# The norm ahead of an FFN in two halves, the output projection in an order that suits it, and the next chunk's gate and up products ahead of the LoRA products

## The reference

```python
x = x + attention(layernorm(x), ctx)          # 16 heads of 32, causal; "x1" below
h = layernorm(x)
logits = h @ W_router                         # 8 experts, top 2 -> weights w (rows x 8)
gate = h @ W_gate + lora(h, sA_gate, sB_gate) + expert_lora(h, A_gate, B_gate, w)
up   = h @ W_up   + lora(h, sA_up, sB_up)     + expert_lora(h, A_up, B_up, w)
hidden = silu(gate) * up                      # 1376 columns, padded to 11 chunks of 128
x = x + hidden @ W_down + lora(...) + expert_lora(...)   # "x2"
x = x + softmax(layernorm(similarity(layernorm(x), ctx)))  # "x3"
x = x + sparse_ffn(layernorm(x))              # 64 experts, top 8
```

## Time and profile before

| | us |
|---|---|
| median of 3 runs | 1436.13 (1434.3 to 1439.93) |
| the profiled execution's own time | 1430.09 |
| its span in the profile | 1428.3 |
| PE busy | 1220.8 |
| DVE busy | 742.1 |
| ACT busy | 504.6 |
| POOL busy | 503.5 |

### The profile page before, as it was taken

The page is one execution under the profiler, slowest core; times in us unless marked ns, Lnnn a source line. Parts: engine busy times, 40 slices in busy tenths (PEclk is TensorE's granted clock), DMA queues, the critical chain, the costliest instruction groups (busy, mean ns, idle before and its releaser), DMA issues. The chain is left out here.

```text
span 1428.3 us, 19290 instructions
## 1 busy us (share of the span) xinstructions
PE 1220.8 (85%) x6510; PEld 891.9 (62%) x6510; DVE 742.1 (52%) x1427; ACT 504.6 (35%) x1145; POOL 503.5 (35%) x533
## 2 busy tenths in 40 slices
PE   0788999887999987799998779999349999999990
PEld 0567777655777765577776557777145666666660
DVE  6674645576576658568666847443641222222220
ACT  1681322565322167422216643121222233323320
POOL 2520333633033373303346330221005455555541
PEclk9999999998999999899999999999658999999995
DMA  7002221000242100033200002641417999999957
GB/s 263 1 1 91 81 108 54 0 1 31 91 141 81 54 1 1 31 115 116 107 28 1 1 31 114 233 153 42 199 68 247 338 338 353 355 348 359 276 85 132
DMA packets 45600, 181.07 MB, mean 127 GB/s; under 512 B 6412, under 2 KB 9484, under 8 KB 36692
## 3 DMA queue, kind: packets, MB, share of 16 engines
q1 hardware_dynamic: 30660, 140.23, 26.2%
q0 software_dynamic: 14864, 39.85, 12.2%
HBM read 149.36 MB, written 34.90 MB: 129 GB/s over the span
## 5 line engine op out<-in xcount | busy, mean ns | idle before, releaser
L2001 PE MATMUL PS<-WE,XGT 128*128 128x384 f32 x512 | 195.2, 505 | 1.5 <-DVE HM L1577 0.8
L656 POOL CAST HH<-HID 128x512 fp32r<-128x512 f32 x44 | 34.0, 773 | 343.2 <-DVE HID L1483 343.2
L786 ACT ACTIVATE P<-PS,NM 128x512 f32<-128x512 f32 (+3 forms) x256 | 132.0, 534 | 50.4 <-DVE NM L1194 49.2
L1600 PE MATMUL PS<-XTH,WHI 128*128 128x512 f32 x352 | 142.9, 406 | 1.0 <-ACT SIL L929 1.0
L1436 DVE TENSOR_TENSOR WLO<-WRAW,WHI 128x584 fp32r<-128x584 f32 (+1 forms) x88 | 109.7, 1247 | 62.8 <-ACT WHI L915 57.0
L1601 PE MATMUL PS<-XTL,WHI 128*128 128x512 f32 x352 | 140.3, 399 | 0.0
L1602 PE MATMUL PS<-XTH,WLO 128*128 128x512 f32 x352 | 140.3, 399 | 0.0
L915 ACT ACTIVATE WHI<-WRAW 128x1280 fp32r<-128x1280 f32 x44 | 56.2, 1277 | 207.0 <-DMA WRAW<-in_ffn 204.1
L2001 PEld LDWEIGHTS PS<-WE,XGT 128*128 128x128 f32 x512 | 88.2, 192 | 57.8 <-issue 23.5
L1194 DVE TENSOR_REDUCE NM<-PS 128x2 f32<-128x1024 f32 (+2 forms) x96 | 98.6, 1041 | 44.8 <-PE PS L1609 44.3
L1660 PE MATMUL PS<-ident,P 128*128 128x128 f32 x640 | 97.5, 289 | 22.8 <-ACT P L786 12.8
(11 more groups left out here) (269 smaller groups left out, 2748.0 us busy)
## 6 DMA issues: line engine op xcount, KB each, us to landing
WE<-in_we SPq DMA_DIRECT2D x64, 1152.0 KB
WRAW<-in_ffn SPq DMA_DIRECT2D x44, 932.0 KB, 4.6
acc<-HN SPq DMA_DIRECT2D x17, 256.0 KB, 4.6
XIN<-in_x SPq DMA_DIRECT2D x4, 1024.0 KB, 9.2
out<-X SPq DMA_DIRECT2D x4, 1024.0 KB, 4.2
out<-acc POOLq DMA_DIRECT2D x1, 4096.0 KB, 23.3
hx<-HN SPq DMA_DIRECT2D x3, 1152.0 KB, 8.7
CTX<-in_ctx SPq DMA_DIRECT2D x4, 256.0 KB, 6.7
```

Source lines behind the costliest of these rows:

```text
L786: act.activation(prob(t, n), PS[:, c0:c0 + (t + 1) * P], ACT.Exp, bias=NM[:, c:c + 1], accum_out=SSUM[:, c:c + 1]).then_inc(S["p_ready"], 1)
L1600: pe.matmul(dst, a[0], b_[0], start=first, stop=False, **kw)
L2001: mm = pe.matmul(bank(2 + s % 2, 0, 2 * F1), XGT[s % 2][:, k, :], WE[s][:, k * 2 * F1:(k + 1) * 2 * F1], start=(k == 0), stop=(k == KC - 1))
```

## The change

1. *Output projection.* PE makes pieces 0 to 2 of tiles 0, 1, 2, the context product, piece 3 of these three, the keys' transposition, and then tile 3 whole.
2. *Norm in two halves.* DVE sums and takes statistics for tiles 0 and 1 and posts their variances, then for tiles 2 and 3. POOL raises each half to -1/2 and normalises its two tiles itself (`first_norm`). The norms of a batch count 5 instead of 4.
3. *Head of the FFN.* The transposed tiles go to banks 6, 7, 4, 5. PE interleaves transposes and projections. DVE subtracts chunk 0's weights between tiles 1 and 2.
4. *Chunk 1.* Its gate and up products go to banks 4 and 5 and stand ahead of the LoRA products of chunk 0; both chunks' LoRA products follow. Its weights are split before. Banks 6, 7, 2 are zeroed behind them, banks 4 and 5 within `down(0)`, which takes tiles 2, 3, 0, 1 and waits for chunk 1's HID in between.
5. *Loads and side work.* SP loads chunks 0 and 1 as soon as attention's last product is made. The next batch's front work goes to chunks 2, 3 and 4, 5, 6, 8; `gates_rest` goes behind chunk 1.

```diff
+NORMS = 5
+TURNED_BANK = (6, 7, 4, 5)
+GATE_BANK, UP_BANK = {1: 4}, {1: 5}
+    FRONT_Q = (4, 5, 6, 8)
...
                 sp.wait_ge(S["pv_ps"], 1 + G * (b + 1))
                 alone(sp, "sp")
-                sp.wait_ge(S["x1_ready"], 1 + NT * (b + 1))
-                alone(sp, "sp")
                 sp.dma_start(WRAW[0][:, :], w["ffn"][0:P, :]).then_inc(w_loaded[0], 16)
                 sp.dma_start(WRAW[1][:, :], w["ffn"][P:2 * P, :]).then_inc(w_loaded[1], 16)
                 if not last:
+                    sp.wait_ge(S["x1_ready"], 1 + NT * (b + 1))
                     sp.wait_ge(S["ctxT_ps"], 1 + b + 1)
...
+            def power(b, n, t0=0, t1=NT):
+
+                pool.wait_ge(S["norm_in"], 1 + NORMS * b + n)
+                pool.tensor_tensor(sm[1][:, t0:t1], sm[0][:, t0:t1], mhalf[:, t0:t1], ALU.pow).then_inc(S["norm_out"], 1)
...
+            def first_norm(a):
+
+                for n, (t0, t1) in ((1, (0, 2)), (2, (2, 4))):
+                    power(a, n, t0, t1)
+                    normed(a, n, XN, "xn_ready", t0, t1)
...
-                        if i == 0 and not last:
-                            front_power(b + 1, d)
-                    if not last:
-                        front_q(b + 1, i)
+                        f = 2 * i + d
+                        if f in (2, 3) and not last:
+                            front_power(b + 1, f - 1)
+                        if f in FRONT_Q and not last:
+                            front_q(b + 1, FRONT_Q.index(f))
...
+                act.wait_ge(S["op_ps"], 1 + NT * b + 1)
+                wg_hi(0, 0, b * N0 + 1)
                 act.wait_ge(S["op_ps"], 1 + NT * (b + 1))
...
-                wg_hi(0, 0, b * N0 + 1)
...
                 def chunk(f, slot, next_loads):
 
-                    if next_loads is not None:
+                    if next_loads is not None and f > 1:
                         act.wait_ge(S["up_ps"], 1 + b * NF + f)
                         wg_hi(f + 1, 1 - slot, next_loads)
...
                     silu(f)
+                    if f == 1:
+                        act.wait_ge(S["up_ps"], 1 + b * NF + 1)
+                        wg_hi(2, 0, next_loads)
+                wg_hi(1, 1, b * N1 + 1)
...
                 dve.wait_ge(S["out_stored"], 16 * (a + 1))
-                stats(row_x, x1, "x1_ready", NT * a)
-                variances(a, 1, EPS_LN)
-                normed(a, 1, XN, "xn_ready")
-                dve.wait_ge(S["xn_ready"], 1 + NT * (a + 1))
+                for t0, n in ((0, 1), (2, 2)):
+                    x1(t0)
+                    x1(t0 + 1)
+                    stats_x1(t0)
+                    step.need(stats_x1(t0 + 1))
+                    aggregate(t0, t0 + 2)
+                    variances(a, n, EPS_LN, t0, t0 + 2)
...
+                turned_rest(0)
+                turned_rest(1)
                 w_rest(0, 0, 0, WD, "wg_hi", "wg_lo")
+                turned_rest(2)
+                turned_rest(3)
...
+                w_rest(1, 1, 0, WD, "wg_hi", "wg_lo")
                 for h in range(2):
                     dve.wait_ge(S["lx_hi"], 1 + 2 * b + h + 1)
...
                 chunk(0, 0)
+                chunk(1, 1)
                 if b > 0:
                     gates_rest(b - 1)
...
+                pe.wait_ge(S["oT_lo"], 1 + (G - 1) * (a + 1))
+                for t in range(NT - 1):
+                    if t == 1:
+                        inverse(G - 1)
+                    projected_out(t, 0, KC - 1)
+                pe.wait_ge(S["ctxT_sb"], 1 + a + 1)
+                pe.matmul(bank(0), wk[:, :], UN[:, :], start=True, stop=True).then_inc(S["kvT_ps"], 1)
+                pe.wait_ge(S["oT_last_lo"], 1 + a + 1)
+                for t in range(NT - 1):
+                    projected_out(t, KC - 1, KC).then_inc(S["op_ps"], 1)
                 pe.wait_ge(S["kv_act"], 1 + a + 1)
                 for t in range(NT):
                     mm = pe.transpose(bank(0, t * P, (t + 1) * P), KVT[:, t * P:(t + 1) * P], ident[:, :])
                 mm.then_inc(S["kv_ps"], 1)
+                projected_out(NT - 1, 0, KC).then_inc(S["op_ps"], 1)
...
+                turned(0)
+                turned(1)
+                projection(0)
+                turned(2)
+                projection(1)
+                turned(3)
+                projection(2)
+                projection(3)
...
-                    for t in range(NT):
+                    for t in (2, 3, 0, 1):
+                        if f == 0 and t == 0:
+                            pe.wait_ge(S["hid_ready"], 1 + b * NF + 2)
+                            clear(4, 5)
...
+                gate_up(1, 1, "weights")
                 pe.wait_ge(S["lx_lo"], 1 + 2 * (b + 1))
                 gate_up(0, 0, "lora")
-
-                for bk in (4, 5, 6, 7, 2):
-                    pe.matmul(bank(bk), zrow[:, 0:P], zrow[:, :], start=True, stop=False, skip_group_check=True)
+                gate_up(1, 1, "lora")
+                clear(6, 7, 2)
                 for f in range(NF - 1):
-                    gate_up(f + 1, (f + 1) % 2)
+                    if f > 0:
+                        gate_up(f + 1, (f + 1) % 2)
                     down(f, f % 2)
```

More of the change, by code:

```diff
@@ L687, in _ @@
             split_output(0, G - 2)
-            power(0, 1)
+            first_norm(0)
             for b in range(B - 1):
@@ L904, in ffn @@
             def ffn(b):
-                act.wait_ge(S["op_ps"], 1 + NT * (b + 1))
-                for t in range(NT):
-                    act.wait_ge(S["xT_ps"], 1 + NT * b + t + 1)
-                    act.activation(XTH[:, :, t * P:(t + 1) * P], bank(4 + t).rearrange("p (k q) -> p k q", k=KC),
-                                   ACT.Copy).then_inc(S["xT_hi"], 1)
                 N0, N1 = NF // 2 + 1, NF // 2
@@ L915, in wg_hi @@
                     act.activation(WHI[slot][:, 0:WD], WRAW[slot][:, 0:WD], ACT.Copy).then_inc(S["wg_hi"], 1)
+                act.wait_ge(S["op_ps"], 1 + NT * b + 1)
                 wg_hi(0, 0, b * N0 + 1)
+                act.wait_ge(S["op_ps"], 1 + NT * (b + 1))
+                for t in range(NT):
+                    act.wait_ge(S["xT_ps"], 1 + NT * b + t + 1)
+                    act.activation(XTH[:, :, t * P:(t + 1) * P], bank(TURNED_BANK[t]).rearrange(
+                        "p (k q) -> p k q", k=KC), ACT.Copy).then_inc(S["xT_hi"], 1)
                 if b > 0:
@@ L1472, in ffn, with chunk @@
                     "lg_ready", b + 1)
-                def chunk(f, slot, last=False, meanwhile=lambda: None):
-                    if not last:
+                def chunk(f, slot, last=False):
+                    if not last and f > 1:
                         w_rest(f + 1, 1 - slot, 0, WD, "wg_hi", "wg_lo")
                     w_rest(f, slot, WD, WCOLS, "wd_hi", "wd_lo")
-                    meanwhile()
                     dve.wait_ge(S["sil_ready"], 1 + b * NF + f + 1)
@@ L1482, in chunk @@
                     dve.wait_ge(S["hl_ready"], 1 + b * NF + f)
[L1483 removed]
+                    sig(dve.tensor_tensor(HID[:, :], SIL[:, :], bank(UP_BANK.get(f, 1)), ALU.mult), "hid_ready",
+                        b * NF + f + 1)
+                    if f == 1:
+                        w_rest(2, 0, 0, WD, "wg_hi", "wg_lo")
+                w_rest(1, 1, 0, WD, "wg_hi", "wg_lo")
                 for h in range(2):
@@ L1894, in gate_up, with clear @@
                                   False, True).then_inc(S[done], 1)
+                def clear(*banks):
+                    for bk in banks:
+                        pe.matmul(bank(bk), zrow[:, 0:P], zrow[:, :], start=True, stop=False, skip_group_check=True)
                 def down(f, slot):
```

122 lines of the change are left out of this document (59 added, 63 removed).

## The result

The changed kernel takes 1441.27 us (median of 20 runs, 1437.66 to 1443.67), the kernel before 1436.35 beside it (20 runs, 1430.15 to 1441.88). The ratio is 1.0029, interval 1.0016 to 1.0042. The prediction was 1432.7, 0.9976 of before: the time moved the other way, and 1441.27 lies just outside its range of 1424.5 to 1440.5. 1.0029 is less than the half per cent that one measurement can tell from no change, but its interval leaves 1 out, and a second measurement (the last experiment) gave 1.0020 [1.0002, 1.0038].

A forecast was written before the change was run, and what follows sets the result against it. TensorE was taken to bound the kernel, with waits to win only in four attention-to-FFN passages. Batch 0's -2.2 and the others' -1.2 gave -3.4 us, profiled 1426.7, median 1432.7 (0.9976); range 1424.5 to 1440.5.

The forecast's parts named there:

- What bounds the kernel: Whole kernel: TensorE busy 1220.8 of 1428.3 us, without waits inside the FFN's 11 chunks, so only the attention-to-FFN passages can gain.
- Part 1, batches 1 to 3: Passage up to the small projections' end: order costs 0.0, POOL slowed by DVE's subtraction 0.6; +0.6 us a batch.
- Part 1, batch 0: Same stretch in batch 0: -2.0 from the order, +0.6 POOL contention, +0.5 low clock; -0.9 us.
- the term for batch 0's clock: Batch 0 up to the projections' end: TensorE's clock still low after idling, adding 0.5 us (0 to 1.5).
- Part 2, order and waits: Projections' end to chunk 2: 21.2 us, with 1.1 waiting for HL, instead of 23.4 (batch 0: 23.7); contention adds 0.4.
- Part 2, the clock's fall: Behind the HL wait, before chunk 2: the low clock returns, partly under the pause, costing 0.8 us (0 to 1.5) a batch.
- the stretch is about as long as before: LoRA products, zeroings and pause before chunk 2: 4.7 us beside 4.5 before, so the clock's fall was expected again.
- The edit touches only these passages: Outside the four attention-to-FFN passages, one per batch, the time was taken as unchanged: no term.
- The last step: Profiled time to median: the result stands to its profile as before's 1436.13 to 1430.09, turning 1426.7 into 1432.7 us.
- Full clock: Rival: 2.4 GHz holds from projections' end to chunk 2, without either contention; -10.6 us in all, 1425.5 us; chance 0.21.
- No gain: Rival: the pause only moves, HL wait 2 us, clock fall 1.5, norm contention 1.0; about +2, 1438 us; chance 0.25.
- POOL's norm as the cost: Rival: POOL's normalising passes slow down beside DVE; 1.3 us longer each gives +15 us, 1451 us; chance 0.10.

The follow-up runs named there:

- the last experiment: The changed kernel itself, with nothing further altered, measured and profiled once more against the kernel before: 1439.29 us, ratio 1.0020.
- experiment 6: The changed kernel plus unread filler products around the XN transposes only, none before the first down product: 1437.71 us, ratio 0.9988 to the kernel before.
- experiment 1: The changed kernel without chunk 1's reordering; norm halves, output projection order and early loads stay: 1437.9 us, ratio 1.0024 to the kernel before.
- experiment 7: The changed kernel plus six unread filler products ahead of the first down product only: 1434.37 us, ratio 0.9974 to the kernel before.
- experiment 5: The kernel before plus unread filler products ahead of the XN transposes and of the first LoRA products: 1431.91 us, ratio 0.9949 to the kernel before.
- experiment 4: The changed kernel with the normalising passes on VectorE instead of GpSimd, still in halves: 1441.92 us, ratio 1.0054 to the kernel before.
- the control: Another name for experiment 5: the kernel before with unread filler products in TensorE's waits, 1431.91 us, ratio 0.9949.

## Why the prediction was wrong, step by step

**What bounds the kernel: right.** PE still has no wait inside the 11 chunks, and all of the difference in the passages is PE's waits and its clock.

**Part 1, batches 1 to 3: right.** Predicted +0.6, measured +0.61 in all three. POOL's power for two columns takes 0.72 (predicted 0.7), a pass 2.07, and the subtraction beside the second pair costs it 0.9 (0.6 of 0 to 1.2).

**Part 1, batch 0: wrong, and the first step that failed.** The step is the term for batch 0's clock. Predicted -0.9: 2.0 us for the earlier XN, against +0.6 and +0.5 "for batch 0's clock". Measured +1.8. The last transposes, small projections and the first products ran at 1.2 GHz for some 17 us; with the clock held the same front takes 26.57 (experiment 6), so the term of 0.5 (0 to 1.5) measures 3.4. Before's long pause had a fall that ended before the projections were half done (6.8 us of low clock); with a pause in pieces it lasted through them (17.1 us).

**Part 2, order and waits: right in mechanism, 0.3 us off.** The sum of products, transposes and waits was 21.2, with 0.4 for contention 21.6; held at full clock it measures 21.9. The wait for HL came as described, 1.50 us and not 1.1: HID's chain from 897.84 to 901.15 takes 3.3 us where 2.95 was taken; HH beside the down-weight subtraction takes 1.07 us instead of 0.61. That is the contention that had 0.4, so the wait came as summed, and the 0.3 left over are spread over the products. But at equal clock this part wins little: the old order takes 22.1 without its fall (experiment 1), so 0.2 us a batch was won where the sum had 0.5 (23.4 - 1.3 - 21.6). The other half of the predicted -1.0 was a fall that was to cost 0.8 where before's cost 1.3. The wait for LXL is gone, chunk 2's weights are never late, the table load stands at no place in the chain.

**Part 2, the clock's fall: the term that was mis-sized.** "0.8 of 0 to 1.5", from 1.3 in before. Measured, as middle less 21.9: 4.0 in batch 0, 1.5 in batch 1, 0 in batch 2, 3.5 in batch 3, 9.0 us in all where 3.2 stood. (Of batch 0's 4.0 some 1.7 belong to the front's fall, which reaches 3.6 us into chunk 0: experiment 7, with that and no later fall, has 23.56.) The step was "the stretch is about as long as before", so the fall comes again, and partly under the pause. It did not follow: the same 1.50 us wait is followed by nothing, by a short fall or by one that lasts past chunk 2's start, and before's rows had four nearly equal cases. Nor was the stretch's pause what counted: before's fall stayed when the pause was filled (experiment 5) and was absent with it (experiment 1). What sets a fall's place and length stays open. The bound of 1.5 was read from one size of fall as if it were the largest.

**The sum.** The passages had -3.4, and measure +6.3: 2.7 is batch 0's front, 5.8 the falls in the middle (1.7 of it the front's), 1.2 the 0.3 us by which part 2 is longer in each batch. The clock thus makes some 8.5 of the 9.7 us between forecast and profile, and that explains the sign. "The edit touches only these passages" put all else at nothing; the profiles have 6.2 us more outside them, and whose they are is open. The last step, that the median stands to the profiled execution as before, hid another: before's profiled 1430.09 is a good-clock execution of a kernel that has such in half of its runs. The change's cost at the median is not only the difference of two profiles but also how often an execution gets the good clock.

**The rivals.** Full clock came true in batch 2 alone, and by fillers. The mechanism of "No gain" came nearest: a longer wait for HL and the clock's fall at its full price, but the price was above the one that it allowed. POOL's norm as the cost fell with experiment 4. None of them had a fall that costs more than 1.5 us, and falls that cost 2.3 to 3.5 us decided.

## What to carry to other kernels

When TensorE has short waits, a move that shifts or splits them is priced by the clock around them as well, and a trace that shows four falls of one length doesn't bound the length of the next. Compare two orders by stretches in which neither has a fall; unread products in the waits can give such stretches, but look whether they did: here they held the clock in some places and not in others. A wait exchanged for another of its length wins nothing. Then look for an order that leaves no wait at all: here twelve independent products laid over the chain HID to HL brought 0.6 to 0.8 per cent against the kernel before, where the norm's halves cost 0.6 us a batch. And take the clock of every execution, not of one profile; the kernel before has two groups of executions 6 us apart, and their shares differ from one block of runs to the next by more than most changes are worth.

## What the runs showed of the hardware

The low clock can outlast the wait that it follows by far: in batch 0 of the changed kernel it stayed at 1.2 GHz for some 17 us, with PE fully busy in windows such as 138 to 139. It can also come with hardly a wait: in the control at 0.18 us, as in before at 1.33. A wait of 1.50 us was followed by none, by a short and by a long fall in the same execution. VectorE and GpSimd were slower side by side, by amounts that depend on the pair: POOL's pass of 2.07 us took up to 3.11 beside DVE's subtraction of two SBUF tensors, its CAST of 0.61 us took 1.07 and, beside the next subtraction, 1.80. Source view of POOL's pass in the changed kernel:

```profile
L636 POOL TENSOR_SCALAR XN<-X,MV,sm x28: 2064/2077/3109, 125.2 to 877.1; 128x512 f32<-128x512 f32 x28
```
